# VectorE scans one tile ahead of the product with C in layer 0 of a Mamba and mixture-of-experts kernel

## The chip, the cores and the metric

The kernel runs on one core of a Trainium2 chip. Times are device microseconds (us) of that core. The engines are TensorE (PE in the rows, PEld for its weight loads), VectorE (DVE), ScalarE (ACT), GpSimd (POOL) and SyncE (SP), which here issues the DMAs. Each engine works its instructions off in order; they wait for one another on semaphores. The kernel before takes 2349.91 us, the median of three runs (2349.65 to 2363.62).

## The reference

Two layers follow one another. Layer 0, which the change touches, adds to x a Mamba block of LN(x) and a gated feed-forward network of 8 experts. What matters of it:

```python
delta = softplus(dt @ dt_w + dt_b)           # 8192 tokens, 256 channels
def step(h, (d_t, x_t, B_t, C_t)):           # 16 states per channel, sequences of 256 tokens
    h = exp(d_t * A) * h + (d_t * x_t) * B_t
    y = sum over the states of h * C_t
y = (ys + xi * D) * silu(z);   mamba = x + y @ out_proj
ffn = sum over 8 experts of gate_e * (relu(x @ W1_e + b1_e) @ W2_e + b2_e)
```

Layer 1 (attention, then a second mixture of experts) is not touched.

## The kernel before

Layer 0 works in 16 iterations of 512 tokens. The states of an iteration are 32 tiles of 128 x 512, and each iteration has 32 slots h, one tile each. The functions `slot(h, it, par)` and `fore(h, n, q)` of each engine are called in turn by `pipeline` (L205): slot h does the work of tile h of iteration `it`, fore h does a piece of the front (projections, convolution, gates) of the next iteration. So each engine's order is written out, and iteration it's last slot is followed by slot 0 of it + 1. `place(k)` gives tile k's half, state group q and block. Iterations 1 to 12 are the body of a hardware loop of two iterations (`Fori`, L227).

Through one tile go these steps:

- ScalarE, `make_da(k, it)` (L541 on): dA = exp(A * delta) into bank k % 3 of the PSUM tile dA (L555). It runs two slots ahead: slot h calls `make_da(h + 2, it)`. It waits until VectorE's product of the tile that had this bank is done: `prod_done.at(it, LAST_IN_BANK.get(k, k - 2))`. `prod_done.at(it, n)` is reached when n products of iteration `it` are done, so tile k waits for product k - 3. 32 tiles do not divide by 3 banks, and at the seam `LAST_IN_BANK = {0: -1, 1: 0, 2: -2}` holds: tile 0 waits for product 30 of the iteration before, tile 1 for product 31, the last, and tile 2 for product 29.
- GpSimd, `make_dbx(s, it)` (L685): dBx for two tiles at once, from DX and BC, which DMAs have loaded. The DMAs for BC wait in `load_states` (L285, L266).
- VectorE, `scan(k, it)` (L845): the recurrence, in place in dA.
- VectorE, `times_c(k, it)` (L854): PR = dA * C, the product of this text. It waits for the scan of the same tile (`scan_done`), and for a tile with k % 4 == 0 also for TensorE's sum that frees PR.
- TensorE, `add_states(b, it)` (L395): sums four products into YS. `evacuate` (L860) takes YS away.

Beside this TensorE runs the experts: `up` (L374) in slots 0, 1, 4, 5, ..., two products each, `down` (L383) in slots 2, 3, 6, 7, ... `up` with index k waits for ScalarE's `relu` (L564) with index k - 2. ScalarE's slots with an `up` are relu, make_da, relu. In slots 3, 7, ..., 31 it calls `apply_gate` (GD, L571) behind make_da. The front's pieces that the prediction speaks of: TensorE x0 (L447) and x1 (L451) in fore 0 and 4, where x1 waits for VectorE's first convolution (L914, fore 3), xproj (L458) in fore 10; VectorE's soft, lg (fore 19) and lnw (L933, fore 20).

Of the kernel before, what the change touches and what calls it, by code (L numbers as in the profile page):

```python
# [29 lines left out]
TILES = HALF * NQ * DB  # L30
# [20 lines left out]
def layer0(nc, ctx, t, dram, scratch):  # L51
# [149 lines left out]
    def place(k):  # L201

        return k // (NQ * DB), k // DB % NQ, k % DB
# [586 lines left out]
    def _(dve):  # L790
# [48 lines left out]
        def scan(k, it):  # L839

            dve.wait_ge(da_ready.sem, da_ready.at(it, k + 1))
            if k % 2 == 0:
                dve.wait_ge(dbx_ready.sem, dbx_ready.at(it, k // 2 + 1))
            h = dA[:, k % 3, :]
            nc.vector.tensor_tensor_scan(h, h, dBx[:, k // 2 % 2, k % 2, :], 0.0, ALU.mult, ALU.add).then_inc(scan_done.sem, 1)  # L845

        def times_c(k, it):

            q = place(k)[1]
            dve.wait_ge(scan_done.sem, scan_done.at(it, k + 1))  # L850
            if k % DB == 0:
                dve.wait_ge(sumf.sem, sumf.at(it, k // DB - 1))
                dve.wait_ge(bc_loaded[q // 2].sem, bc_loaded[q // 2].at(it, 16 * NQ))
            nc.vector.tensor_tensor(PR[:, k % (2 * DB), :], dA[:, k % 3, :], BC[:, q // 2, 2 + q % 2, :], ALU.mult).then_inc(prod_done.sem, 1)  # L854

        def evacuate(h, it, par):

            dve.wait_ge(sumf.sem, sumf.at(it, NQ * h + NQ))
            dve.wait_ge(outf.sem, outf.at(it - 1, 1))
            nc.vector.scalar_tensor_tensor(y[:, h, :], xi[:, par, h, :], Dp[:, h:h + 1], YS[:], ALU.mult, ALU.add).then_inc(ev_done.sem, 1)  # L860

        def store(it, par):

            dve.wait_ge(outf.sem, outf.at(it, 1))
            dve.wait_ge(acc_done.sem, acc_done.at(it, E0))
            dve.wait_ge(xo_stored.sem, xo_stored.at(it - 1, 16))
            dve.wait_ge(restat.sem, restat.at(it - 1, 1))
            nc.vector.tensor_tensor(XO[:], FRO[:].rearrange("p (j d) -> p j d", d=D), FF[:, par], ALU.add).then_inc(x_done.sem, 1)

        def restatistic(it):  # L870

            dve.wait_ge(x_done.sem, x_done.at(it, 1))
            for j in range(J0):
                last = nc.vector.bn_stats(stats[:, bass.ds(it * J0 + j, 1), :].rearrange("p o s -> p (o s)"), XO[:, j, :])
            last.then_inc(restat.sem, 1)

        def slot(h, it, par, first=False, final=False, last_front=False):

            scan(h, it)
            if h == DVE_AT["ev0"]:  # L880
                evacuate(0, it, par)
            if not first:
                if h == DVE_AT["ev1"]:
                    evacuate(1, it - 1, 1 - par)
                if h == DVE_AT["store"]:
                    store(it - 1, 1 - par)
            times_c(h, it)
            if h == DVE_AT["stat"] and not first:
                restatistic(it - 1)

        def end(it, par):
            evacuate(1, it, par)
            store(it, par)
            restatistic(it)
# [4 lines left out]
        def fore(h, n, q):  # L899
# [54 lines left out]
            if h == DVE_AT["z1"]:  # L954
# [3 lines left out]
                nc.vector.scalar_tensor_tensor(z1[:, q, :], tanhz[:, 1, :], 1.0, FRO[:], ALU.add, ALU.mult).then_inc(z_done.sem, 1)  # L958

        pipeline(fore, lambda: None, slot, end, dve, between)  # L960
        dve.wait_ge(restat.sem, restat.at(IT0 - 1, 1))

# [843 lines left out]
```

## Time and profile before

| | us |
|---|---|
| median of 3 runs | 2349.91 |
| the profiled execution | 2364.9 |
| its span | 2363.1 |
| first and last scan of layer 0 start at | 99.7 and 1471.5 |
| busy, share of the span: PE, DVE, ACT, POOL | 83%, 76%, 56%, 55% |

Starts are counted from the span's start. A row of a timeline has start, duration, engine, line, operation, out<-in, and in brackets how long the engine sat idle before it and what ended the wait. A PE matmul of float32 stands as two records, so "UP x4" is two calls of `up`. A row of a table by windows has start:end and length, then busy time (x instructions) of PE, PEld, DVE, ACT and POOL, then TensorE's granted clock as a share of full speed, the DMA share and GB/s. Busy time of TensorE is modelled: an engine that is 95% busy by it is not at its peak.

### The profile page before, as it was taken

The numbers are of one execution on the slowest core, as the hardware profiler recorded it, in microseconds if no ns is written. First come the engines' busy times: TensorE is split into PE (matmuls) and PEld (weight loads), VectorE is DVE, ScalarE is ACT, GpSimd is POOL, SyncE is SP. The second block draws the span as 40 slices with busy tenths as digits, with TensorE's granted clock in tenths as the row PEclk, the third lists the DMA queues.
The fourth block names the chain that finished last, engine by engine and source line by source line (L and its number), as shares of the span: only waits on it lengthen the run. The fifth ranks groups of instructions, "written<-read, shape, count | busy, mean of one in ns | idle before, by whom it ended". The sixth has DMA issues, their size and how long they took to land. (4 is left out here: it accounts for less than half of the span.)

```text
span 2363.1 us, 42425 instructions
## 1 busy us (share of the span) xinstructions
PE 1969.3 (83%) x13497; PEld 1138.0 (48%) x13562; DVE 1789.5 (76%) x2995; ACT 1329.3 (56%) x2381; POOL 1303.1 (55%) x1004
## 2 busy tenths in 40 slices
PE   1799999999999999999999999389999999985220
PEld 0456555555555555555555555244555555542120
DVE  3598888988988988988888888276777777767305
ACT  1576676677677677677677675045555555552000
POOL 0486776776876776776777776222223222212650
PEclk9799999999999999999999999589999999997555
DMA  7523532532542541541541550533333333310117
GB/s 185 131 72 70 126 82 65 128 87 58 130 100 51 128 105 41 126 109 37 126 113 38 116 125 6 149 98 97 100 100 99 104 107 98 100 62 3 29 39 216
DMA packets 196935, 221.69 MB, mean 94 GB/s; under 512 B 28856, under 2 KB 139488, under 8 KB 192672
## 3 DMA queue, kind: packets, MB, share of 16 engines
q1 hardware_dynamic: 194720, 215.49, 35.5%
q0 software_dynamic: 2048, 4.16, 0.6%
q8 instruction: 82, 1.34, 0.2%
q14 instruction: 85, 0.70, 0.1%
HBM read 165.40 MB, written 54.24 MB: 93 GB/s over the span
## 5 line engine op out<-in xcount | busy, mean ns | idle before, releaser
L685 POOL TENSOR_TENSOR dBx<-REP,BC 128x1024 f32<-128x1024 f32 x256 | 603.1, 2359 | 288.4 <-DVE dA L845 245.8
L845 DVE TENSOR_TENSOR_SCAN dA<-dA,dBx 128x512 f32<-128x512 f32 x512 | 626.4, 1224 | 113.9 <-ACT dA L555 63.0
L374 PE MATMUL UP<-xnT,W 128*128 128x512 f32 x1024 | 517.7, 625 | 52.5 <-ACT hT L564 40.4
L383 PEld LDWEIGHTS DN<-W,hT 128*128 128x128 f32 x4096 | 469.4, 192 | 110.0 <-issue 99.7
L383 PE MATMUL DN<-W,hT 128*128 128x128 f32 x4096 | 496.1, 278 | 0.3 <-ACT GD L571 0.3
L564 ACT ACTIVATE hT<-UP,b 128x512 f32<-128x512 f32 x512 | 355.2, 694 | 88.5 <-PE UP L374 84.5
L555 ACT ACTIVATE dA<-REP,A 128x512 f32<-128x512 f32 x512 | 354.1, 695 | 69.9 <-DVE PR L854 69.6
L854 DVE TENSOR_TENSOR PR<-dA,BC 128x512 f32<-128x512 f32 x512 | 353.3, 690 | 31.5 <-DVE dA L845 18.8
L1528 DVE TENSOR_REDUCE NM<-S 128x4 f32<-128x1024 f32 (+1 forms) x192 | 234.9, 1223 | 129.1 <-PE S L1218 106.1
L374 PEld LDWEIGHTS UP<-xnT,W 128*128 128x128 f32 x1024 | 180.5, 195 | 280.0 <-issue 145.7
L1379 ACT ACTIVATE PT<-S 128x1024 f32<-128x1024 f32 x192 | 197.0, 1026 | 140.6 <-PE S L1232 108.3
L571 ACT ACTIVATE GD<-DN,gate 128x128 f32<-128x128 f32 x512 | 145.3, 366 | 137.2 <-PE DN L383 136.7
L1413 POOL TENSOR_TENSOR t<-t 128x512 f32<-128x512 f32 x32 | 40.6, 1267 | 324.6 <-DVE t L1474 324.6
L695 POOL TENSOR_TENSOR FF<-FF,GD 128x512 f32<-128x512 f32 x128 | 162.5, 1270 | 6.1 <-ACT GD L571 6.1
L395 PE MATMUL YS<-PR,fold 128*32 128x512 f32 x1024 | 139.4, 617 | 0.5 <-DVE PR L854 0.5
L914 DVE SCALAR_TENSOR_TENSOR xch<-FRO,convw,xch 128x510 f32<-128x510 f32 (+2 forms) x96 | 71.5, 745 | 30.9 <-ACT xch L611 28.6
L1254 PE MATMUL OT<-PT,V 128*9 128x256 f32 x1024 | 82.3, 383 | 0.0
L1206 PE MATMUL S<-maskq,identb 128*128 128x512 bf16 x126 | 38.6, 387 | 50.8 <-DMA QS<-s_parts 50.7
L1625 ACT COPY XGT<-TR 128x512 f32<-128x512 f32 x8 | 4.7, 585 | 127.6 <-remote 58.5
L1373 ACT COPY OSB<-OT 128x512 f32<-128x512 f32 x64 | 37.6, 588 | 68.7 <-PE OT L1256 68.7
L1419 POOL TENSOR_TENSOR SPL<-t,SPL 128x512 bf16<-128x512 f32 x32 | 44.7, 1396 | 47.6 <-ACT SPL L1385 47.6
L1710 DVE COPY YB<-EO 128x512 f32<-128x512 f32 x8 | 5.5, 691 | 85.4 <-remote 79.6
(242 smaller groups left out, 2858.0 us busy)
## 6 DMA issues: line engine op xcount, KB each, us to landing
REP<-s_delta SPq DMA_DIRECT2D x128, 256.0 KB, 7.8
REP<-s_dx SPq DMA_DIRECT2D x128, 256.0 KB, 7.2
BC<-s_b SPq DMA_DIRECT2D x128, 256.0 KB, 8.3
s_parts<-SPL SPq DMA_DIRECT2D x32, 384.0 KB, 2.8
s_dx<-tz SPq DMA_DIRECT2D x16, 512.0 KB, 3.2
WE<-in_L_ffn_we SPq DMA_DIRECT2D x32, 256.0 KB, 3.0
s_y<-zeros SPq DMA_DIRECT2D x32, 256.0 KB, 3.1
YC<-s_y SPq DMA_DIRECT2D x16, 512.0 KB, 6.0
```

The costliest lines, as they stand in the source:

```text
L374: nc.tensor.matmul(UP[k % 2][:], W1[:, e % E0, f * P:(f + 1) * P], xnT[:, q, :], start=True, stop=True).then_inc(upf.sem, 1)
L383: last = nc.tensor.matmul(DN[:, j * P:(j + 1) * P], hT[:, e % 2, f, j * P:(j + 1) * P], W2[:, e, f, :], start=(f == 0), stop=(f == FB - 1))
L395: last = nc.tensor.matmul(YS[CB * j:CB * j + CB, :], fold[:], PR[:, (DB * b + j) % (2 * DB), :], start=(q == 0), stop=(q == NQ - 1), tile_ ...
L555: nc.scalar.activation(dA[:, k % 3, :], DR[:, h, j, :], ACT.Exp, scale=A[:, h, j, q:q + 1]).then_inc(da_ready.sem, 1)
L564: nc.scalar.activation(hT[:, e % 2, f, :], UP[k % 2][:], ACT.Relu, bias=b1[:, e % E0, f:f + 1]).then_inc(relu_done.sem, 1)
L571: last = nc.scalar.activation(GD[:, e % 2, j, :], DN[:, j * P:(j + 1) * P], ACT.Copy, scale=gate[:, par, j, e:e + 1])
L685: nc.gpsimd.tensor_tensor(dBx[:, s % 2], DX[:, h, j:j + 2, :], BC[:, q // 2, q % 2, :].unsqueeze(1).to_broadcast([P, 2, T0]), ALU.mult).th ...
L695: nc.gpsimd.tensor_tensor(FF[:, par], FF[:, par], GD[:, e % 2], ALU.add).then_inc(acc_done.sem, 1)
L845: nc.vector.tensor_tensor_scan(h, h, dBx[:, k // 2 % 2, k % 2, :], 0.0, ALU.mult, ALU.add).then_inc(scan_done.sem, 1)
L854: nc.vector.tensor_tensor(PR[:, k % (2 * DB), :], dA[:, k % 3, :], BC[:, q // 2, 2 + q % 2, :], ALU.mult).then_inc(prod_done.sem, 1)
L1379: nc.scalar.activation(PT[:, u // 3, u % 3, :], S2[:].rearrange("p b w -> p (b w)"), ACT.Exp, scale=SCALE).then_inc(exp_done.sem, 1)
L1528: nc.vector.tensor_reduce(NM[:, 0 if a == 0 else 1, :].rearrange("p (r i) -> p r i", r=2)[:, :, heads], S1[:].rearrange("p r (j k) -> p r ...
```

## The change

In each VectorE slot h the scan of tile h now stands ahead of the product of tile h - 1. In slot 0 it is followed by product 31 of the iteration before, and after the last iteration `end` makes the last product. No instruction is added or removed, and no other engine's code changes; the waits of each instruction are the same.

```diff
-            times_c(h, it)
+            if h:
+                times_c(h - 1, it)
+            elif not first:
+                times_c(TILES - 1, it - 1)
             if h == DVE_AT["stat"] and not first:
                 restatistic(it - 1)
 
         def end(it, par):
+            times_c(TILES - 1, it)
             evacuate(1, it, par)
             store(it, par)
             restatistic(it)
```

VectorE from the start of the loop body, which is slot 0 of an iteration, before (`TENSOR_TENSOR PR` is a product; ISA and REGISTER_ALU are waits and their arithmetic; the scan is named SCALAR_TENSOR_TENSOR dA here):

```order
L227 UNCONDITIONAL_BRANCH
L227 ISA
L843 ISA
L845 SCALAR_TENSOR_TENSOR dA<-dA,dBx 128x512
L852 ISA
L853 ISA
L854 TENSOR_TENSOR PR<-dA,BC 128x512
L841 REGISTER_ALU
L845 SCALAR_TENSOR_TENSOR dA<-dA,dBx 128x512
L854 TENSOR_TENSOR PR<-dA,BC 128x512
```

VectorE at the same place with the change:

```order
L227 UNCONDITIONAL_BRANCH
L227 ISA
L843 ISA
L845 SCALAR_TENSOR_TENSOR dA<-dA,dBx 128x512
L850 ISA
L854 TENSOR_TENSOR PR<-dA,BC 128x512
L841 REGISTER_ALU
L845 SCALAR_TENSOR_TENSOR dA<-dA,dBx 128x512
L852 ISA
L853 ISA
L854 TENSOR_TENSOR PR<-dA,BC 128x512
```

The product behind scan 0 waited at L852 and L853 for PR and BC, as product 0 does; now these two waits stand behind scan 1, and the product behind scan 0 is product 31 of the iteration before.

## Rows read from the trace of the kernel before

**Rows 1.** One iteration in the table by windows: iteration 6, from scan 0 to scan 0
```profile
618.80:706.00 87.20, 81.58 (x440) 48.05 (x438) 76.13 (x91) 61.74 (x116) 65.02 (x43) 0.98 0.40 94
```

**Rows 2.** VectorE's timeline over the seam of iterations 5 and 6
```profile
614.93 0.69 DVE L854 TENSOR_TENSOR PR<-dA,BC 128x512 f32<-128x512 f32 x1
618.82 1.23 DVE L845 TENSOR_TENSOR_SCAN dA<-dA,dBx 128x512 f32<-128x512 f32 x1 [3.20 <-POOL dBx L685]
```

**Rows 3.** GpSimd's timeline and SyncE's DMA issues ahead of scan 0 of iteration 6
```profile
616.43 2.35 POOL L685 TENSOR_TENSOR dBx<-REP,BC 128x1024 f32<-128x1024 f32 x1 [2.39 <-DMA BC<-s_b]
...
604.10 13.24 SPq L266 DMA_DIRECT2D BC<-s_b  x8
```

**Rows 4.** ScalarE's timeline over the same seam
```profile
616.58 0.70 ACT L555 ACTIVATE dA<-REP,A 128x512 f32<-128x512 f32 x1
617.88 1.14 ACT L571 ACTIVATE GD<-DN,gate 128x128 f32<-128x128 f32 x4 [0.61 <-PE DN L383]
618.89 0.70 ACT L564 ACTIVATE hT<-UP,b 128x512 f32<-128x512 f32 x1
619.46 0.72 ACT L555 ACTIVATE dA<-REP,A 128x512 f32<-128x512 f32 x1
620.08 0.71 ACT L564 ACTIVATE hT<-UP,b 128x512 f32<-128x512 f32 x1
```

**Rows 5.** TensorE's timeline of iteration 6: slots 0, 1 and 4, and xproj
```profile
617.68 1.88 PE L374 MATMUL UP<-xnT,W 128*128 128x512 f32 x4
619.40 1.02 PE L447 MATMUL FRO<-xrT,inproj 128*128 128x512 f32 x2
620.26 1.88 PE L374 MATMUL UP<-xnT,W 128*128 128x512 f32 x4
622.07 1.07 PE L395 MATMUL YS<-PR,fold 128*32 128x512 f32 x8
...
629.34 1.12 PE L451 MATMUL FRO<-xrT,inproj 128*128 128x512 f32 x2 [0.71 <-DVE xch L914]
...
647.51 1.91 PE L458 MATMUL FRO<-xi,xproj 128*40 128x512 f32 x4
```

**Rows 6.** TensorE's timeline of iteration 3
```profile
358.34 1.98 PE L374 MATMUL UP<-xnT,W 128*128 128x512 f32 x4 [1.79 <-issue]
...
363.67 1.06 PE L395 MATMUL YS<-PR,fold 128*32 128x512 f32 x8
...
388.12 1.91 PE L458 MATMUL FRO<-xi,xproj 128*40 128x512 f32 x4
```

**Rows 7.** VectorE's timeline: scan 0 of iterations 1, 3, 4, 7 and 15
```profile
183.18 1.23 DVE L845 TENSOR_TENSOR_SCAN dA<-dA,dBx 128x512 f32<-128x512 f32 x1 [3.59 <-POOL dBx L685]
...
358.51 1.23 DVE L845 TENSOR_TENSOR_SCAN dA<-dA,dBx 128x512 f32<-128x512 f32 x1 [3.70 <-POOL dBx L685]
...
445.68 1.23 DVE L845 TENSOR_TENSOR_SCAN dA<-dA,dBx 128x512 f32<-128x512 f32 x1 [2.92 <-POOL dBx L685]
...
706.02 1.23 DVE L845 TENSOR_TENSOR_SCAN dA<-dA,dBx 128x512 f32<-128x512 f32 x1 [3.86 <-POOL dBx L685]
...
1403.52 1.23 DVE L845 TENSOR_TENSOR_SCAN dA<-dA,dBx 128x512 f32<-128x512 f32 x1 [3.23 <-POOL dBx L685]
```

**Rows 8.** VectorE's timeline: a product behind its own scan, an evacuation behind another's
```profile
671.93 1.23 DVE L845 TENSOR_TENSOR_SCAN dA<-dA,dBx 128x512 f32<-128x512 f32 x1
673.36 0.69 DVE L854 TENSOR_TENSOR PR<-dA,BC 128x512 f32<-128x512 f32 x1 [0.19 <-DVE dA L845]
...
624.61 1.22 DVE L845 TENSOR_TENSOR_SCAN dA<-dA,dBx 128x512 f32<-128x512 f32 x1
625.74 0.72 DVE L860 SCALAR_TENSOR_TENSOR y<-xi,Dp,YS 128x512 f32<-128x512 f32 x1
```

**Rows 9.** TensorE's timeline behind a wait of 2.6 us in slot 21 of iteration 5
```profile
589.37 2.95 PE L374 MATMUL UP<-xnT,W 128*128 128x512 f32 x4 [2.61 <-ACT hT L564]
592.25 1.94 PE L395 MATMUL YS<-PR,fold 128*32 128x512 f32 x8
```

**Rows 10.** The table by windows for the second half of that stretch
```profile
591.50:594.00 2.50, 2.50 (x9) 0.20 (x8) 2.27 (x6) 2.50 (x6) 2.50 (x2) 0.50 0.35 114
```

## The prediction

> **What bounds the kernel now.** I read the table by windows first, then the timelines of VectorE, ScalarE and TensorE over the seam between two iterations. In one iteration of 87.2 us TensorE is busy for 81.6 us, VectorE for 76.1, GpSimd for 65.0 and ScalarE for 61.7 [rows 1]. TensorE is nearest to full, and VectorE has 11 us of slack. Part of that slack sits at a fixed place: each iteration's scan 0 comes 3 to 4 us after VectorE has run out of work, for it waits for GpSimd's dBx [rows 2, 7], which waits for the DMA of BC [rows 3]. So an iteration has one fixed point, the start of scan 0, which I call T0, and the reader is to see that VectorE's speed does not set it. T0 of iteration 1 is at 183.18 and of iteration 15 at 1403.52 [rows 7]: 14 iterations of 87.16 us.
>
> What sets T0 hangs on the front: TensorE's xproj and, 30 us later, ScalarE's and GpSimd's work on delta and its DMAs. From xproj to the next T0 it takes 706.02 - 647.51 = 58.5 us in iteration 6 and 445.68 - 388.12 = 57.6 in iteration 3 [rows 5 to 7]. I take 58.0 as rigid. The mean offset of xproj from T0 is then 87.16 - 58.0 = 29.2 us. Whatever moves xproj against T0 moves the end.
>
> **What the swap does to VectorE alone.** A product behind its own scan starts 673.36 - 671.93 = 1.43 us after the scan's start in the slower cases and 1.25 in the others (1.22 of scan, 0.03 idle). An instruction that does not need the scan starts 625.74 - 624.61 = 1.13 us after it [rows 8]. The swap puts an independent product behind each scan, so VectorE gains 0.12 to 0.30 us for each of 512 pairs, 61 to 154 us in all, by these rows. Nearly all of it is free time ahead of T0, where it adds to the 3 us that VectorE waits anyway. What stays is the product ahead of lnw in slot 20, on the way to delta: I book 0.3 us less from xproj to T0, so 57.7.
>
> The Trainium skill, VectorE: DVE Perf Modes, section "The DRAIN you can't avoid", says that a semaphore after each VectorE operation costs nothing extra, because the pipe's flush stands between two of them anyway. By it the swap would save VectorE nothing, and my total below would be some 4 us higher; the rows disagree, with 1.25 and 1.43 us against 1.13, and I go by them.
>
> **What it adds: a wait at the seam.** Product h - 1 now ends a scan later. Inside an iteration ScalarE's make_da(h + 2) needs just this product, so its lead over VectorE shrinks from two tiles to one. At the seam the lead was already one tile shorter, since tile 1 takes the bank of tile 31: ScalarE in slot 31 makes dA of tile 1 and waits for product 31. Before, that product ended at 614.93 + 0.69 = 615.62, before T0 = 618.82 [rows 2], and ScalarE made the tile at 616.58 [rows 4]. Now product 31 stands behind scan 0, which waits for GpSimd, and ends at T0 + 1.13 + 0.69 = T0 + 1.82. Queued behind make_da(1) on ScalarE are GD and the relus that TensorE's next `up` waits for. Step by step, with the spacings of the rows:
>
> - make_da(1) starts at T0 + 1.86 (before: T0 - 2.24), GD 0.6 later at 2.5, the relu of slot 0 another 618.89 - 617.88 = 1.0 later at 3.5, done with 0.70 at T0 + 4.2. make_da(2) starts 0.57 after that relu did, the second relu 0.62 later at 4.7, done at T0 + 5.4 [rows 4].
> - TensorE's slot 1 needs the first of these relus for its first `up` and the second for its second. Before it started at 620.26 = T0 + 1.4 [rows 5]. Now the first starts at T0 + 4.2, the second at T0 + 5.4, and the sum YS behind them at T0 + 6.4 (before: T0 + 3.3).
> - In iteration 6 TensorE loses 0.7 us of that lead in slot 4 anyway, where x1 waits for the convolution [rows 5]. Where it does not, xproj follows YS by 388.12 - 363.67 = 24.4 us [rows 6]. So xproj comes at T0 + 6.4 + 24.4 = T0 + 30.8. Later waits in slots 2 to 12 (make_da(6) and make_da(7) behind the two convolutions move by 1.5 to 5 us) fall into the time that TensorE is then late, by my walk through the slots, and cost nothing more.
>
> **A second price, the clock.** Slot 0's `up` and x0 end at 619.40 + 1.02 = T0 + 1.6 [rows 5], so TensorE idles from there to T0 + 4.2, 2.6 us. The same idle of 2.61 us stands in slot 21, and behind it `up` took 2.95 us and YS 1.94, against 1.88 and 1.07 [rows 5, 9], at a granted clock of 0.50, the level of 1.2 GHz [rows 10]. That is 1.9 us; I take 1.5, for the second `up` waits for its relu anyway. Xproj is then at T0 + 32.3. In the five iterations behind a jump back of the loop (six trips, two iterations each) TensorE arrives 1.8 us later, as in iteration 3, where slot 0 starts at 358.34 = T0 - 0.2 [rows 6, 7] and x0 is done some 2.9 us later. There it idles 1.5 us and I book no slow clock.
>
> **The sum.** Five iterations of 30.8 + 57.7 = 88.5 us and nine of 32.3 + 57.7 = 90.0 are 1252.5 us, against 14 x 87.16 = 1220.2: 32 us more. The last iteration has the seam too, and less front work to hide it: 2 more. That is 34 us. The profiled execution, 2364.9 us, would become 2399. It lies 15 us over the median of the runs, 2349.9; from that median the forecast is **2384 us**, 1.4% slower.
>
> Bounds: without any slow clock each seam costs 88.5 - 87.2 = 1.3 us, 20 in all: 2370. With the full 1.9 in all 15 seams and nothing absorbed later, YS is 3.1 us late in each: 15 x (3.1 + 1.9) = 75, less 4 for lnw: 2421. VectorE's moved waits for PR and BC cost nothing: TensorE's sums were done long before, and the second half of BC, asked for only when product 31 is done (so 5 us later, T0 + 2 instead of T0 - 3), has until tile 8 in slot 7.
>
> **The rivals.**
>
> *The seam is absorbed.* TensorE waits anyway: in slot 4 for the convolution (0.71 us in iteration 6), in slot 21 for ScalarE (2.6 us). If those shrink by what the seam adds, the time stays, 2345 to 2370. For it: the mean xproj offset of 29.2 shows little dependence on when YS comes (T0 + 3.3 and 5.2 give 28.7 and 29.6). Against it: the wait in slot 21 is for ScalarE's chain of table loads, which itself starts from TensorE's front products, so it moves along. Chance 0.2.
>
> *Faster: VectorE's pairs do pay.* If T0 is set through VectorE (lnw, the convolutions of slots 3 and 4, xi) more than I think, each iteration gains the 0.12 us of the pairs between those points, 12 to 20 pairs with some at 0.3: 2 to 4 us per iteration, 15 times, 30 to 60 us: 2290 to 2320. It decides when ScalarE's relus wait less than 0.7 us longer at the seam, that is when scan 0 is no longer held back by dBx. Against it: scan 0 waited 2.9 us and more for dBx in each seam shown [rows 2, 7]. Chance 0.06.
>
> *Slower by more.* ScalarE's shorter lead bites in slots 4, 5, 9 and 22 to 29 as well: VectorE's gate work of fore 22 now stands ahead of product 22, and GD and two relus behind make_da come 0.5 us later. A further 1 to 2 us per iteration: 2400 to 2415. Chance 0.14. My forecast has the remaining 0.6.
>
> **How the numbers follow.** The predicted time is that of the likeliest case. The range leaves out the faster case and the tails of the others: 2358 to 2408 us. A measurement can tell about 1% from no change, 23.5 us. Above 2373.4 lie four fifths of the forecast's 0.6 and the 0.14 of the worse case and a little of the absorbed one: 0.65 slower. Faster by over 1% is 0.06. The rest, 0.29, is within 1%.
>
> **What would show it.** VectorE: product 31 right behind scan 0, ending at T0 + 1.8, with no idle between scan and product. ScalarE: make_da(1) at T0 + 1.9 with over 4 us of idle ahead of it that ends with a product; before, there was none. TensorE: idle of about 2.6 us in slot 1 that ends with a relu, in 15 places, and a granted clock of 0.5 behind most of them; xproj at T0 + 31 to 32; iterations of 88.5 to 90 us. The forecast is wrong if xproj stays at T0 + 29, or if the idle in slot 21 shrinks by what slot 1 gains. VectorE's scan 0 must still wait for dBx; if not, the fixed point is gone and with it the sum.

## The result and the profile after

The changed kernel takes 2403.86 us, the median of four runs (2398.01 to 2407.06); the kernel before took 2350.14 beside it (2349.65 to 2363.62, four runs). The ratio is 1.0209, with a 95% interval of 1.0173 to 1.0245: slower, as forecast, and inside the range (2358 to 2408), but by 54 us where 34 were forecast.

The profiled execution took 2398.0 us (span 2396.2), that of before 2364.9. These two differ by only 33 us, since the part behind layer 0, which the change does not touch, happened to be 17 us shorter in this execution. So layer 0 is compared by itself, by the view of one line, that of the product (duration min/median/max, then the start of the first and the last of 512), before and then after:

```profile
L854 DVE TENSOR_TENSOR PR<-dA,BC x512: 675/691/693, 101.0 to 1472.7; 128x512 f32<-128x512 f32 x171
```

```profile
L854 DVE TENSOR_TENSOR PR<-dA,BC x512: 666/673/687, 103.5 to 1523.0; 128x512 f32<-128x512 f32 x171
```

The last product starts 50.3 us later, which is the 54 of the runs within their spread. The page of the changed kernel, busy time of the engines and the product's group:

```profile
PE 1977.3 (83%) x13497; PEld 1132.4 (47%) x13562; DVE 1749.9 (73%) x2995; ACT 1331.6 (56%) x2381; POOL 1302.6 (54%) x1004
...
L854 DVE TENSOR_TENSOR PR<-dA,BC 128x512 f32<-128x512 f32 x512 | 344.6, 673 | 0.0
```

VectorE is 39.6 us less busy than before (1749.9 against 1789.5), and the group of products shows no wait any more (0.0). VectorE was helped, and the kernel is slower: it is not the engine that bounds. The trace counts six records more than before (42431 against 42425), one more wait of VectorE per trip of the loop; its 2995 operations are the same.

VectorE over the same seam as [rows 2], now T0 = 640.51:

```profile
636.52 0.67 DVE L854 TENSOR_TENSOR PR<-dA,BC 128x512 f32<-128x512 f32 x1
640.51 1.23 DVE L845 TENSOR_TENSOR_SCAN dA<-dA,dBx 128x512 f32<-128x512 f32 x1 [3.31 <-POOL dBx L685]
641.65 0.68 DVE L854 TENSOR_TENSOR PR<-dA,BC 128x512 f32<-128x512 f32 x1
643.08 1.23 DVE L845 TENSOR_TENSOR_SCAN dA<-dA,dBx 128x512 f32<-128x512 f32 x1 [0.76 <-ACT dA L555]
...
728.92 1.23 DVE L845 TENSOR_TENSOR_SCAN dA<-dA,dBx 128x512 f32<-128x512 f32 x1 [3.33 <-POOL dBx L685]
```

Scan 0 still waits for dBx, product 31 follows at T0 + 1.14, and VectorE then has a wait of its own, for tile 1. ScalarE, the rows that answer to [rows 4]:

```profile
642.36 0.69 ACT L555 ACTIVATE dA<-REP,A 128x512 f32<-128x512 f32 x1 [3.28 <-DVE PR L854]
642.99 1.12 ACT L571 ACTIVATE GD<-DN,gate 128x128 f32<-128x128 f32 x4
643.98 0.70 ACT L564 ACTIVATE hT<-UP,b 128x512 f32<-128x512 f32 x1
644.55 0.71 ACT L555 ACTIVATE dA<-REP,A 128x512 f32<-128x512 f32 x1
645.16 1.42 ACT L564 ACTIVATE hT<-UP,b 128x512 f32<-128x512 f32 x2
```

And TensorE, answering to [rows 5]:

```profile
640.08 1.88 PE L374 MATMUL UP<-xnT,W 128*128 128x512 f32 x4
641.80 1.02 PE L447 MATMUL FRO<-xrT,inproj 128*128 128x512 f32 x2
644.74 2.31 PE L374 MATMUL UP<-xnT,W 128*128 128x512 f32 x4 [1.92 <-ACT hT L564]
646.98 1.07 PE L395 MATMUL YS<-PR,fold 128*32 128x512 f32 x8
...
671.44 1.05 PE L458 MATMUL FRO<-xi,xproj 128*40 128x512 f32 x2
```

Tile 1 at T0 + 1.85, the relu at T0 + 3.47, slot 1 of TensorE at T0 + 4.23, YS at T0 + 6.47, xproj at T0 + 30.9, the next T0 88.4 us on. The chain of the prediction stands there to some 0.1 us, but without a slow clock: TensorE idled 1.9 us, not 2.6. It is so in eight of the nine iterations that are not behind a jump back of the loop (I call them plain). Their idles were 1.65 to 2.63 us, and the `up` behind them took 2.31; the window of the longest, in iteration 13, has a granted clock of 1.00. Only in iteration 1, behind 2.39 us, was it slow: 3.35 us at 0.57.

Behind a jump back it looks otherwise. Iteration 5 (T0 = 548.34), ScalarE and then TensorE:

```profile
550.18 0.69 ACT L555 ACTIVATE dA<-REP,A 128x512 f32<-128x512 f32 x1 [3.81 <-DVE PR L854]
550.81 1.12 ACT L571 ACTIVATE GD<-DN,gate 128x128 f32<-128x128 f32 x4
554.32 0.69 ACT L564 ACTIVATE hT<-UP,b 128x512 f32<-128x512 f32 x1 [2.39 <-issue]
```

```profile
548.99 1.98 PE L374 MATMUL UP<-xnT,W 128*128 128x512 f32 x4 [1.45 <-issue]
550.80 1.02 PE L447 MATMUL FRO<-xrT,inproj 128*128 128x512 f32 x2
555.06 3.52 PE L374 MATMUL UP<-xnT,W 128*128 128x512 f32 x4 [3.24 <-ACT hT L564]
558.51 1.06 PE L395 MATMUL YS<-PR,fold 128*32 128x512 f32 x8
```

Between GD and the relu ScalarE waits 2.39 us for nothing that the profile names: it is at the jump. TensorE's idle is 3.24 us, and the `up` behind it takes 3.52 us. Slot 1 starts at T0 + 6.7 and xproj at T0 + 34.6, against 4.2 and 30.9 in iteration 6: 2.5 us from the jump and 1.2 from the slow clock. The table by windows shows its clock there (columns as in [rows 1]):

```profile
555.10:558.60 3.50, 3.50 (x8) 1.17 (x12) 1.94 (x3) 2.36 (x4) 0.67 (x1) 0.56 0.99 202
558.60:560.60 2.00, 2.00 (x17) 1.16 (x18) 1.96 (x3) 1.96 (x3) 0.03 (x1) 1.00 1.08 222
```

Layer 0's account, from the starts of scan 0 and of the last product (us):

| | before | after | more | forecast |
|---|---|---|---|---|
| up to T0 of iteration 0 | 99.7 | 101.2 | 1.5 | 0 |
| iteration 0 | 83.5 | 87.0 | 3.6 | 0 |
| 9 iterations of 1 to 14 not behind a jump | 782.9 | 800.4 | 17.5 | 27 |
| 5 iterations behind a jump (3, 5, 7, 9, 11) | 437.4 | 459.6 | 22.2 | 5 |
| iteration 15, to the last product | 69.2 | 74.7 | 5.5 | 2 |

### The profile page after: what moved, and what is told of

Same layout as the page of the kernel before. It is cut to its first block and busy times, and to the rows that moved or that the text cites. A ratio compares the mean times of both kernels' runs of the same rounds, so it can differ in the third digit from the quotient of the medians.

```text
span 2396.2 us, 42431 instructions
## 1 busy us (share of the span) xinstructions
PE 1977.3 (83%) x13497; PEld 1132.4 (47%) x13562; DVE 1749.9 (73%) x2995; ACT 1331.6 (56%) x2381; POOL 1302.6 (54%) x1004
## 5 line engine op out<-in xcount | busy, mean ns | idle before, releaser
L374 PE MATMUL UP<-xnT,W 128*128 128x512 f32 x1024 | 526.2, 629 | 101.9 <-ACT hT L564 89.0
L564 ACT ACTIVATE hT<-UP,b 128x512 f32<-128x512 f32 x512 | 355.2, 694 | 57.5 <-PE UP L374 43.1
L854 DVE TENSOR_TENSOR PR<-dA,BC 128x512 f32<-128x512 f32 x512 | 344.6, 673 | 0.0
L374 PEld LDWEIGHTS UP<-xnT,W 128*128 128x128 f32 x1024 | 174.5, 194 | 344.5 <-ACT hT L564 220.1
L395 PEld LDWEIGHTS YS<-PR,fold 128*32 128x32 f32 x1024 | 20.5, 110 | 105.6 <-issue 54.3
```

Source lines behind the costliest of these rows:

```text
L374: nc.tensor.matmul(UP[k % 2][:], W1[:, e % E0, f * P:(f + 1) * P], xnT[:, q, :], start=True, stop=True).then_inc(upf.sem, 1)
L395: last = nc.tensor.matmul(YS[CB * j:CB * j + CB, :], fold[:], PR[:, (DB * b + j) % (2 * DB), :], start=(q == 0), stop=(q == NQ - 1), tile_ ...
L564: nc.scalar.activation(hT[:, e % 2, f, :], UP[k % 2][:], ACT.Relu, bias=b1[:, e % E0, f:f + 1]).then_inc(relu_done.sem, 1)
```

## The experiments

Each is compared by its time and by the start of its last product, in its own profiled execution, which leaves out what happens behind layer 0. It does not leave out the start: scan 0 of iteration 0 comes at 98.2 to 101.4 us in these executions (before 99.7, the change 101.2), so a difference of two last products holds up to 3 us of that. They were run beside the kernel before, which took 2365 to 2367 us there and not 2350, so a time is to be read by its ratio to those runs, not against the times that were expected.

### The seam alone, and all but the seam

VectorE's calls in slot h, product 31 back in its own slot:

```diff
+            if h:
+                times_c(h - 1, it)
+            if h == TILES - 1:
+                times_c(h, it)
```

> Product 31 is made in slot 31 again, right behind product 30; inside an iteration the products still run one scan late. Theory (the seam): ScalarE's tile 1 no longer waits for scan 0, so iterations 1 to 14 fall from a mean of 90.0 us to the 87.2 of before; only iteration 0 keeps its 3.6 us and the last one about 2. Layer 0's last product starts at 1476 to 1480 us (1472.7 before, 1523.0 with the change), the time is 2350 to 2360 us. Rival (the shorter lead of ScalarE inside every iteration, slots 4, 5, 9 and 22 to 29): the seam is a small part, iterations stay at 89 us and more, 2380 to 2400 us.

Measured: 2391.67 us, ratio 1.0109 (1.0082 to 1.0137); the last product starts at 1497.9. Half of the loss went, not all of it. The nine plain iterations fell from a mean of 88.9 to 87.2, beside the 87.0 of before, so there the seam is nearly the whole of it. The shorter lead is not free there, but nearly paid back: xproj comes at T0 + 29.5, before at 29.0 in the mean of the nine, and the rest of the iteration is 0.3 us shorter. Iteration 0 kept 86.9. But the five behind a jump still took 89.1 to 92.9 us, 457.6 together against 459.6 with the change, which neither theory had. ScalarE in iteration 7 (T0 = 714.77):

```profile
713.91 1.14 ACT L571 ACTIVATE GD<-DN,gate 128x128 f32<-128x128 f32 x4 [0.61 <-PE DN L383]
721.45 0.69 ACT L564 ACTIVATE hT<-UP,b 128x512 f32<-128x512 f32 x1 [6.39 <-issue]
```

6.4 us at the jump. The relu's input, TensorE's first `up` of slot 0, started at 716.82 (TensorE had stood 2.95 us at its own jump) and was done a microsecond later, so some 2.8 us of the 6.4 would have been waited anyway, and 3.6 are the jump's alone. So the jump is a price of its own.

The other half of the pair keeps the order of before and moves product 31 alone:

```diff
+            if h == 0 and not first:
+                times_c(TILES - 1, it - 1)
+            if h < TILES - 1:
+                times_c(h, it)
```

> The order of before in slots 0 to 30; only product 31 moves behind scan 0 of the next iteration. Theory (the seam): nearly the whole loss is here: ScalarE's tile 1 starts at T0 + 1.9, iterations behind a jump back take about 92 us, the others 89; the last product starts at 1508 to 1518 us and the time is 2388 to 2400 us. Iteration 0 is at its 83.5 us of before. Rival (shorter lead inside an iteration): 2352 to 2370 us.

Measured: 2428.79 us, ratio 1.0252 (1.0223 to 1.0280); last product at 1538.3, beyond the band, and 15 us later than with the whole change. Iteration 0 is at 83.8. That moving one product of 32 costs all of the loss and more supports the seam; that it costs more needs the next rows, TensorE at the seam of iteration 4 (T0 = 458.54):

```profile
456.59 1.88 PE L374 MATMUL UP<-xnT,W 128*128 128x512 f32 x4
458.31 1.02 PE L447 MATMUL FRO<-xrT,inproj 128*128 128x512 f32 x2
462.77 3.47 PE L374 MATMUL UP<-xnT,W 128*128 128x512 f32 x4 [3.44 <-ACT hT L564]
```

Here TensorE comes to slot 0 at T0 - 1.95, idles 3.4 us and then runs slowly, as the prediction had it for the change. With the whole change it comes at T0 - 0.43, and the idle of 1.9 us is followed by matmuls at full pace. The same holds over the nine plain seams: with product 31 alone moved, TensorE came to slot 0 at T0 - 0.9 to - 2.7, idled 2.4 to 4.2 us, and ran slowly behind seven of them; with the whole change it came at T0 - 0.2 to - 1.1 and ran slowly behind one. From the timelines, ScalarE's shorter lead has made TensorE late already in slots 24 and 25 (up to 1.4 us of idle before an `up`), and that lateness covers part of the seam's wait and saves the clock. The two kernels differ in nothing but the lead inside the iteration; of the 15 us, 10 lie in the plain iterations and 7.5 in those behind a jump, less 3 in iteration 0.

### What is queued behind tile 1

```diff
+            if h == TILES - 1:
+                apply_gate(s // 2, it, par)
             if not (final and s == SLOTS - 1):
                 make_da(h + 2, it)
...
-            if h % 4 == GATE_AT:
+            if h % 4 == GATE_AT and h != TILES - 1:
                 apply_gate(s // 2, it, par)
```

> The changed kernel, but ScalarE in slot 31 applies the gate (GD, 1.1 us) ahead of tile 1, not behind it. Theory (what is queued behind tile 1 on ScalarE is TensorE's price): the relu of slot 0 comes 1.0 us sooner, TensorE's slot 1 starts at T0 + 3.2 instead of 4.2, each of 15 seams gains 1.0 us: the last product starts 13 to 18 us sooner than 1523.0, the time is 2385 to 2392 us. Rival (TensorE would have waited for something else at that point, or T0 moves): no change from 2404 within 4 us.

Measured: 2401.38 us, ratio 1.0145 (1.0120 to 1.0170) against the 1.0209 of the change; last product at 1506.4, 16.6 us sooner (of which 2.2 lie ahead of iteration 0). TensorE at that seam (T0 = 634.04):

```profile
635.24 1.02 PE L447 MATMUL FRO<-xrT,inproj 128*128 128x512 f32 x2
637.24 2.31 PE L374 MATMUL UP<-xnT,W 128*128 128x512 f32 x4 [0.97 <-ACT hT L564]
```

Slot 1 starts at T0 + 3.2, one GD sooner, as expected. What stands behind the waiting instruction on ScalarE is what TensorE pays for.

### The jump back

Six iterations in the loop body instead of two, in the changed kernel, in the one before, and in the one with the seam undone:

```diff
-        with eng.Fori(0, IT0 // 2 - 2) as i:
-            for k in range(2):
-                iteration(i * 2 + (1 + k), 1 - k)
+        with eng.Fori(0, (IT0 - 4) // 6) as i:
+            for k in range(6):
+                iteration(i * 6 + (1 + k), (1 + k) % 2)
```

> The changed kernel with six iterations in the loop body (two trips, one jump back) instead of two (six trips, five jumps). Theory (a jump back costs what it costs on the path: with the change ScalarE reaches it late and the relu behind it comes 2.4 us later still): the four iterations that lose their jump fall from 92 to 89 us, the last product starts at 1508 to 1514 us instead of 1523.0, the time is 9 to 15 us less than the changed kernel's. Rival (the loop's jumps were priced in before too, and the longer body costs fetches of its own): within 4 us of 1523.0.

> The kernel before with six iterations in the loop body. Theory: its jumps were hidden, since ScalarE reached them 2 us ahead of T0 and TensorE had the time: the last product starts at 1467 to 1473 us (1472.7 with two), the time is the same to 4 us less than before. Rival (a jump back costs 3 us in every kernel): 12 us less.

> Products one scan late inside an iteration, product 31 in slot 31, and six iterations in the body. With two in the body this order lost 25 us in layer 0: 4 in iteration 0, and some 20 in the five iterations behind a jump back, where ScalarE stood 4 to 6.6 us at the jump. Theory (the jump's instruction fetch, slower while the DMAs of BC, DX and DR run): four of five are gone, the last product starts at 1478 to 1485 us instead of 1497.9. Rival (those iterations are long for another reason, the late da of the seam): 1494 us or more.

| | ratio to before (95%) | last product, 2 in the body | 6 in the body |
|---|---|---|---|
| the change | 1.0150 (1.0119 to 1.0182) | 1523.0 | 1510.9 |
| before | 0.9993 (0.9977 to 1.0009) | 1472.7 | 1473.5 |
| seam undone | 1.0035 (1.0019 to 1.0050) | 1497.9 | 1483.4 |

In the order of before four jumps fewer bring nothing (1473.5 is 0.5 us outside its band, but what it was to tell apart it does). In the change they bring 12 us, 3 for each jump, and with the seam undone 14.5. The price of a jump is no constant of the kernel: in the order of before the five iterations behind one are 0.5 us longer than the plain ones with two in the body, but iteration 7 with six in the body, behind the one jump left, took 90.2 us, 3 more than the plain ones there, with ScalarE 4.2 us at the jump. ScalarE's waits at its jump, in the view of waits, changed kernel with two and then with six in the body:

```profile
ACT hT L564 <- issue: 11.9, 5, 2.6
```

```profile
ACT hT L564 <- issue: 2.3, 1, 2.3
```

What ScalarE waits for there stands in the trace's record of DMAs, as transfers of the kind instruction. At each of the five jumps one of 8 KB on queue 14 ends, the last before ScalarE goes on, and ScalarE resumes 1.5 to 1.7 us later, with the change and with the seam undone alike. What differs is when this transfer starts: 0.1 to 0.5 us after ScalarE has come to the jump with the change, 1.6 to 4.3 us after with the seam undone. And the data loads differ: the share in which the core's DMA engines were busy in the 3 us ahead was 0.19 to 0.31 with the change, where the loads of BC begin only when product 31 is done, and 0.93 to 0.95 with the seam undone. So the fetch seems to queue behind the loads; no run varied them by themselves, so this is not shown.

### Whose bank it is

The changed kernel with six in the body, and the three banks taken in turn across iterations, with the plain wait for product k - 3 at the seam too:

```diff
+        return (k + 2 * (turn["it"] + d)) % 3
...
-            act.wait_ge(prod_done.sem, prod_done.at(it, LAST_IN_BANK.get(k, k - 2)))
-            nc.scalar.activation(dA[:, k % 3, :], DR[:, h, j, :], ACT.Exp, scale=A[:, h, j, q:q + 1])
+            act.wait_ge(prod_done.sem, prod_done.at(it, k - 2))
+            nc.scalar.activation(dA[:, bank(k, d), :], DR[:, h, j, :], ACT.Exp, scale=A[:, h, j, q:q + 1])
```

> The changed kernel with six iterations in the body and dA's three banks taken in turn over all iterations (192 tiles divide by 3), so that tile k waits for product k - 3 at the seam too: tile 1 for product 30, and only tile 2 for product 31. Theory (the bank of tile 1 is what makes the seam dear): ScalarE's GD and first relu are free of scan 0, slot 1 of TensorE starts at T0 + 1.5 to 2.5, iterations take 87 to 88 us, the last product starts at 1476 to 1490 us, some 25 us sooner than the changed kernel with the same body. Rival (any lag of the products costs this much, whichever tile waits): within 6 us of that kernel, 1505 us or more.

Measured: 2370.76 us, ratio 1.0014 (0.9998 to 1.0031); last product at 1482.3 against 1510.9 with the fixed banks: 28.6 us from naming the banks otherwise (27.3 counted from each kernel's own scan 0 of iteration 0). ScalarE and TensorE at the seam of iteration 5 (T0 = 535.19; the lines are 13 and 12 further down in this kernel):

```profile
533.40 0.70 ACT L568 ACTIVATE dA<-REP,A 128x512 f32<-128x512 f32 x1
534.71 1.14 ACT L584 ACTIVATE GD<-DN,gate 128x128 f32<-128x128 f32 x4 [0.61 <-PE DN L395]
535.72 0.71 ACT L577 ACTIVATE hT<-UP,b 128x512 f32<-128x512 f32 x1
537.04 0.69 ACT L568 ACTIVATE dA<-REP,A 128x512 f32<-128x512 f32 x1 [0.61 <-DVE PR L867]
```

```profile
536.23 1.02 PE L459 MATMUL FRO<-xrT,inproj 128*128 128x512 f32 x2
537.09 1.02 PE L386 MATMUL UP<-xnT,W 128*128 128x512 f32 x2
538.39 1.13 PE L386 MATMUL UP<-xnT,W 128*128 128x512 f32 x2 [0.28 <-ACT hT L577]
```

Product 31 still runs behind scan 0. But tile 1 no longer waits for it; tile 2 does, with GD and a relu already ahead of it, and TensorE idles 0.28 us. This settles the seam: the price came from the bank of tile 1.

### Iteration 0

The seam undone, six in the body, and iteration 0 in the order of before:

```diff
+            if first:
+                times_c(h, it)
+            elif h:
+                times_c(h - 1, it)
+            if h == TILES - 1 and not first:
+                times_c(h, it)
```

> The run with the seam undone and six iterations in the body (last product at 1483.4 us, iteration 0 of 87.1 us), but iteration 0 in the order of before. Theory (in iteration 0 TensorE has no output product of the iteration before in slot 8 to cover ScalarE's late relus): iteration 0 returns to 83.4 us and the last product starts 3 to 4.5 us sooner, 1479 to 1480.5 us. Rival (iteration 0 is long because of its start-up loads): 86.5 us or more, no change.

Measured: 2370.45 us, ratio 1.0024 (1.0011 to 1.0036). Iteration 0 took 83.9 us instead of 87.1, and the last product starts at 1478.2, 5.2 us sooner, just past the band; 0.6 us of the rest lie ahead of iteration 0 and 1.3 behind it. So nearly all of its 3.6 us are the shorter lead. TensorE in slots 8 and 9 of iteration 0, before and then with the change:

```profile
116.99 1.88 PE L374 MATMUL UP<-xnT,W 128*128 128x512 f32 x4
119.97 2.31 PE L374 MATMUL UP<-xnT,W 128*128 128x512 f32 x4 [1.10 <-ACT hT L564]
```

```profile
118.64 1.88 PE L374 MATMUL UP<-xnT,W 128*128 128x512 f32 x4
123.44 3.23 PE L374 MATMUL UP<-xnT,W 128*128 128x512 f32 x4 [2.92 <-ACT hT L564]
126.60 1.79 PE L395 MATMUL YS<-PR,fold 128*32 128x512 f32 x8
```

In every other iteration slot 8 holds the output products of the iteration before, 4 us of TensorE work that cover ScalarE's late relus. Iteration 0 has none, so it idles 2.9 us there and then runs slowly. That this cover is what the other iterations have was read from the timelines, not tried.

### A better order

Late products only where no relu waits for them. First in slots 0 to 3, with product 3 behind the first convolution and ahead of scan 4:

```diff
+            if h == LAG:
+                times_c(h - 1, it)
             scan(h, it)
...
+            if h >= LAG:
+                times_c(h, it)
+            elif h:
+                times_c(h - 1, it)
```

> The kernel before, but in slots 0 to 3 the scan stands ahead of the product of the tile before, and product 3 follows the first convolution, ahead of scan 4. The seam is as before. Theory: the first convolution ends about 1.1 us sooner after T0, so TensorE's x1, which waits 0.7 to 2.2 us for it in nine of the iterations, starts sooner; T0 to xproj shrinks by about 0.7 us in the nine and nothing is lost elsewhere: 6 to 14 us less, the last product starts at 1459 to 1467 us and the time is 2336 to 2344 us. Rival (T0 to xproj is set by TensorE's own work or by ScalarE): no change, 2347 to 2353 us.

Measured: 2362.89 us, ratio 0.9989 (0.9969 to 1.0008), last product at 1471.5: 1.2 us sooner, or 2.2 counted from scan 0 of iteration 0. Xproj is at T0 + 28.4 instead of 28.7 in most iterations, so, as I read it, x1's wait was mostly taken over by TensorE's own work, and my 6 to 14 us were far too many. Its iterations behind a jump stayed at 87.5 to 89.2 us. So with six in the body:

> Products late by one scan in slots 0 to 3 only, as in the run with lag there (its last product at 1471.5 us, its five iterations behind a jump 1.4 us longer than the rest), and six iterations in the loop body. Theory: the first convolution's gain of 0.3 us per iteration stays and four jumps go: the last product starts at 1463 to 1469 us, the time is 0.1 to 0.5% under before. Rival (fetches within the long body take it back, as with the order of before in that body, 1473.5): 1470 to 1475 us, no change.

Measured: 2359.19 us, ratio 0.9972 (0.9958 to 0.9985), last product at 1467.6. And with late products again from slot 10 on:

```diff
+            if 1 <= h <= 3 or h >= 11:
+                times_c(h - 1, it)
+            if 4 <= h <= 9 or h == TILES - 1:
+                times_c(h, it)
```

> Six iterations in the body; products late in slots 0 to 3 (product 3 ahead of scan 4) and again in slots 10 to 31, with product 31 in slot 31; the order of before in slots 4 to 9, where ScalarE's tiles 6 and 7 would hold up relus. Theory: xproj at T0 + 28.4, as with the lag in slots 0 to 3, and 57.7 us from there to the next T0 (58.0 before): iterations of 86.1 to 86.3 us, the last product starts at 1458 to 1466 us, the time is 0.3 to 0.6% under before. Rival (the late products of slots 10 to 31 hold up ScalarE there, or the long body's fetches eat the gain): 1468 us or more, no change.

Measured: 2355.48 us, ratio 0.9960 (0.9944 to 0.9975), last product at 1467.8, 1.8 us outside its band. Both beat both kernels by a little, 6.6 us in layer 0 against before if each is counted from its own scan 0; against each other the intervals overlap and layer 0 is the same, so the second part shows no gain. In the last of them iteration 7, behind the one jump left, took 91.3 us, 5 more than the rest: that hides what slots 10 to 31 may have brought.

## Why the prediction was right, and where it was short

The direction and its mechanism held, point by point. Scan 0 still waits for dBx, 3.3 us; VectorE gained and the end did not (39.6 us less busy). Tile 1 of the seam waits for product 31 behind scan 0, at T0 + 1.85 (forecast 1.86), slot 1 of TensorE follows at T0 + 4.23 (4.2), YS at T0 + 6.47 (6.4), xproj at T0 + 30.9 (30.8), and the iteration is 57.5 us longer than that (57.7). The banks in turn, with nothing else altered, took 28.6 of the 37.4 us that the change with that body had lost to the same body before.

The second price, the clock, was put to the wrong iterations. I booked 1.5 us for nine plain iterations and none for the five behind a jump. The plain ones came out at 88.3 to 89.8 us, mean 88.9, not 90.0: eight of the nine ran at full clock, and four of the five behind a jump idled long and ran slowly. The idle of iteration 6 was 1.9 us and not 2.6, because TensorE reached the seam 0.7 us later than before: the mechanism of my third rival, ScalarE's shorter lead in slots 22 to 29, was at work, and it hid the clock's price instead of adding to it. The step from idle to clock was weak too. I took it from one slot 21, that of iteration 5; in iterations 4 and 10 of the same trace the same idle of 2.60 us is followed by a granted clock of 1.00. That the plain iterations came out too long in the forecast and those behind a jump too short is why the sum, 34 us, is not further from the 50 of layer 0 than it is: that part is luck.

The failed term is the five iterations behind a jump: forecast 88.5 us, measured 90.9 to 92.3. I had read TensorE's 1.8 us at the jump and booked it as an arrival that shortens the idle. I had not asked what ScalarE does there. It too stands at the jump, 2.2 to 2.6 us; before, it reached the jump 0.3 to 1.7 us ahead of T0, and TensorE's own late arrival covered most of its wait of 1.9 to 3.2 us. With the change it reaches the jump only at T0 + 3.6, with TensorE waiting for the very next relu. So five seams got 2.4 us at the jump, an idle of 2.4 to 3.2 us in four of them, and the slow clock behind it; in the fifth, iteration 11, TensorE was slow already behind its own 1.87 us at the jump. The six-iteration body shows the part that goes with the jumps, 12 us.

The Trainium skill, Runtime: NRT & Kernel Launch, section "Instruction fetch mechanics", says that a taken branch whose target is outside the current window must have its page fetched by DMA before the engine goes on. The trace agrees: ScalarE's wait marked issue, 2.2 to 2.6 us in five places, each with an instruction transfer in it, and four of the five gone with the jumps. I had not used it.

Two small terms were missing or too small. One is iteration 0 with 3.6 us, by my reading because it has no output products to cover late relus. The other is the last iteration, with 5.5 us instead of 2. With product 31 back in its slot and all else as in the change it took 70.4 us to its last product, against 74.7 with the change and 69.2 before, so 4.3 us are the seam. It has no x0 to shorten the idle, which was 3.75 us there, and the `up` behind it took 3.65. Of VectorE's moved waits for PR and BC nothing was seen, as forecast. Of the first rival (the seam is absorbed by waits in slots 4 and 21) only the 0.7 us in slot 4 came true, and was in the sum; the wait of 2.6 us in slot 21 stands as before.

The rule of the Trainium skill, VectorE: DVE Perf Modes, section "The DRAIN you can't avoid", by which the swap saves VectorE nothing, was weighed in the prediction. The rows decide against it here: scan to product is 1.13 to 1.14 us now, against 1.25 and 1.43 [rows 8].

## What to carry to other kernels

When an instruction is moved later on an engine, look for who waits for its completion at the seams of the loop, where the rotation of buffers is irregular: a lag that came out even 31 times of 32 cost 1.7 us an iteration the 32nd time, and renaming the buffers so that the rotation runs through took it away. Then ask what is queued behind the waiter on its engine, a jump back of the loop included. When you price an idle of TensorE, look at the granted clock behind every idle of its kind, not behind one.

## What the runs showed of the hardware

- At a jump back ScalarE stood 2.2 to 2.6 us with the change, but 4.1 to 6.6 us with the seam undone (some of it ahead of its input), in the same place of the code. In both it went on 1.5 to 1.7 us after an 8 KB instruction transfer had ended; with the seam undone, where the DMA engines were 0.93 to 0.95 busy in the 3 us ahead, this transfer started 1.6 to 4.3 us after the jump was reached instead of 0.1 to 0.5. That the loads held it up is likely and was not tried.
- TensorE's granted clock behind an idle does not follow from the length of the idle alone. It ran at its lower level (0.50 and 0.56 granted, the level of 1.2 GHz) behind idles of 2.6 us in slot 21 of iteration 5 before and 3.2 us in iteration 5 of the change, and at 0.57 behind 2.39 us in iteration 1. It ran at full clock (1.00, the level of 2.4 GHz) behind 2.60 us in slot 21 of iterations 4 and 10 before and behind 2.63 us in iteration 13 of the change. At a plain seam the lower level moved xproj from T0 + 30.9 to T0 + 32.2 (iterations 6 and 1).
- A VectorE product behind a scan it does not need took 673 ns on average instead of 690, beside starting 0.12 us sooner or more.
